# Carrying the running sum of gamma times v: by the token place in SBUF and two passes with ones, in place of three passes with gamma

## What is computed

```python
q = _mlp(x, W1q, b1q, W2q, b2q)
k = _mlp(x, W1k, b1k, W2k, b2k)
v = _mlp(x, W1v, b1v, W2v, b2v)
scores = jnp.einsum('bid,bjd->bij', q, k) / scale
scores = scores * mask
out = jnp.einsum('bij,bjd->bid', scores, v)
...
out = (out - mu) * jax.lax.rsqrt(var + LN_EPS) * ln_w + ln_b
```

## Time and profile before

| | us |
|---|---|
| median of 3 runs | 637.05 |
| lowest and highest | 636.82, 637.2 |
| the profiled execution | 638.8 |
| its span | 637.1 |
| TensorE busy | 608.0 |
| VectorE busy | 432.8 |
| ScalarE busy | 415.0 |
| GpSimd busy | 349.1 |

### The profile page before, as it was taken

How to read it: one execution, slowest core, us unless ns; L and a number is a source line. 1 busy time by engine, 2 the same in 40 slices (tenths; PEclk the granted TensorE clock), 3 DMA queues, 4 the chain that set the end, 5 groups by cost and what they waited for, 6 DMA issues and landing times. The chain is left out here.

```text
span 637.1 us, 12373 instructions
## 1 busy us (share of the span) xinstructions
PE 608.0 (95%) x4100; PEld 559.9 (88%) x4100; DVE 432.8 (68%) x943; ACT 415.0 (65%) x921; POOL 349.1 (55%) x359
## 2 busy tenths in 40 slices
PE   3999999999999999999999999999999999979994
PEld 2879999899999998998998999989999999868883
DVE  3467777776777777767767778797655555337784
ACT  2656677677676676776776766676766666434665
POOL 1536675775766776756767666566433333003443
PEclk9999999999999999999999999999999999999997
DMA  7211112112111120121111110030000000031434
...
DMA packets 30158, 30.21 MB, mean 47 GB/s; under 512 B 6158, under 2 KB 26028, under 8 KB 30124
## 3 DMA queue, kind: packets, MB, share of 16 engines
...
## 5 line engine op out<-in xcount | busy, mean ns | idle before, releaser
L564 ACT ACTIVATE h_hi<-bank,bias_col 128x512 fp32r<-128x512 f32 x96 | 66.4, 692 | 40.0 <-PE bank L690 39.4
L486 POOL TENSOR_TENSOR h_lo<-xn_all,h_hi 128x512 fp32r<-128x512 f32 x32 | 41.6, 1301 | 79.5 <-ACT xn_all L566 79.4
L688 PE MATMUL bank<-xnT_hi,w_hi 128*128 128x512 f32 x192 | 78.4, 408 | 5.5 <-DVE xnT_lo L978 5.2
L690 PE MATMUL bank<-xnT_hi,w_lo 128*128 128x512 f32 x192 | 77.0, 401 | 0.0
L689 PE MATMUL bank<-xnT_lo,w_hi 128*128 128x512 f32 x192 | 76.8, 400 | 0.0
L1037 DVE TENSOR_TENSOR state_lo<-bank,state_hi 128x512 fp32r<-128x512 f32 x57 | 39.1, 685 | 44.2 <-ACT state_hi L605 44.0
L1411 PE MATMUL bank<-xn_all,e_tok 128*128 128x257 f32 x256 | 66.4, 382 | 0.1
L1317 ACT ACTIVATE e_tok<-bank,shift,xinv 128x256 f32<-128x256 f32 x64 | 36.1, 564 | 44.8 <-PE bank L1394 24.2
L1491 DVE COPY ET_all<-bank 128x256 f32<-128x256 f32 (+1 forms) x64 | 27.0, 423 | 53.2 <-PE bank L1405 52.7
L492 POOL TENSOR_TENSOR ktok_lo<-xn_all,ktok_hi 128x512 fp32r<-128x512 f32 x32 | 38.1, 1193 | 44.8 <-ACT ktok_hi L581 44.8
L605 ACT CAST state_hi<-bank 128x512 fp32r<-128x512 f32 x57 | 33.5, 587 | 42.0 <-PE bank L807 42.0
...
## 6 DMA issues: line engine op xcount, KB each, us to landing
...
```

The source lines that it names most:

```text
L486: pool.tensor_tensor(h_lo[:, V_SLOT, m, :], hv[:, m, :], h_hi[:, V_SLOT, m, :].bitcast(F32), ALU.subtract).then_inc(hv_split, 1)
L564: nc.scalar.activation(h_hi[:, h_slot(j, n), m, :], ps, ACT.Gelu, bias=bias(n, m))
L688: nc.tensor.matmul(ps, w[0], xs[0], start=start, stop=False, skip_group_check=shared)
L690: return nc.tensor.matmul(ps, w[1], xs[0], start=False, stop=stop, skip_group_check=shared)
```

## The change

gamma times v is no longer multiplied by TensorE. VectorE keeps, for each of the 128 token places (partitions), the sum over the chunks so far of gamma v at this place: v_sum[:, c] is the sum ahead of chunk c (sum_v; close_sum hands it on to the next group). ScalarE casts v_sum two chunks at a time (round_vsum), GpSimd takes the difference (split_vsum), and `carry` brings the sum over the 128 places into the chunk's own output tile with a matrix of ones, which needs no low part: two matmuls instead of three. The first matmul of a tile now starts it afresh, so preload and mark_out are gone, and TensorE waits for z_ready itself. causal shrinks to one copy. The numbers of instructions: 180 matmuls with gamma become 120 with ones; 56 preloads, 16 gam_hi, 16 gam_lo and mark_out go; 60 sums on VectorE, 32 casts on ScalarE and 32 differences on GpSimd come.

```diff
@@ -282,13 +282,15 @@
...
             ku_rows = asb("ku_rows", [P, KC])
-            gam_hi = asb("gam_hi", [P, GT], F32R)
-            gam_lo = asb("gam_lo", [P, GT], F32R)
+            v_sum = asb("v_sum", [P, GT, D])
+            vsum_hi = asb("vsum_hi", [P, GT, D], F32R)
+            vsum_lo = asb("vsum_lo", [P, GT, D], F32R)
+            ones_r = asb("ones_r", [P, P], F32R)
             bias_rows = asb("bias_rows", [3 * KB, P])
...
             lnb_rows = asb("lnb_rows", [P, D])
-            causal = asb("causal", [P, GT, P])
+            causal = asb("causal", [P, P])
             xT_hi, xT_lo = xnT_hi[0], xnT_lo[0]
...
@@ -497,6 +497,12 @@
...
                                        ALU.subtract).then_inc(v_split, 1)
+
+                def split_vsum(g, m):
+                    pool.wait_ge(vsum_rounded, 2 * g + m + 1)
+                    pair = slice(2 * m, 2 * m + 2)
+                    pool.tensor_tensor(vsum_lo[:, pair, :], v_sum[:, pair, :], vsum_hi[:, pair, :].bitcast(F32),
+                                       ALU.subtract).then_inc(vsum_split, 1)
 
                 def body(g, j, ba, attend=True, project=True, settle=True, more=True):
...
@@ -511,6 +517,8 @@
...
                     if project:
+                        if attend:
+                            split_vsum(a, 1)
                         split_hv(g, 1)
...
@@ -522,7 +530,10 @@
...
                         split_v(g, 0)
+                        split_vsum(g, 0)
                         split_v(g, 1)
+                        if not more:
+                            split_vsum(g, 1)
                     if attend and project:
...
@@ -575,7 +586,6 @@
...
                     act.wait_ge(k_biased, GT * g + GT)
-                    nc.scalar.copy(gam_hi[:, :], k_tok[:, :, D]).then_inc(gam_rounded, 1)
                     for m in range(2):
...
@@ -584,11 +594,10 @@
...
 
-                def preload(ba, i):
-
-                    act.wait_ge(carried, CB * ba + i - 1)
-                    act.wait_ge(z_ready, TB * ba + i + 2 - i % 2)
-                    nc.scalar.copy(out_tile(i % GT), out_tile((i - 1) % GT)).then_inc(preloaded, 1)
+                def round_vsum(g, m):
+                    act.wait_ge(v_summed, GT * g + 2 * m + 1)
+                    pair = slice(2 * m, 2 * m + 2)
+                    nc.scalar.copy(vsum_hi[:, pair, :], v_sum[:, pair, :]).then_inc(vsum_rounded, 1)
 
                 def round_v(g, m):
...
@@ -625,11 +634,9 @@
...
                         round_state(ba, i + 1, tail_hi[1])
-                        preload(ba, i + 2)
                         nc.scalar.activation(warm[:, :], warm[:, :], ACT.Exp).then_inc(table_warm, 1)
...
                         round_masked(a)
-                        preload(ba, i + 3)
                         apply_z(act, a - 1, (ja - 1) % 2, (0, 1))
...
@@ -639,8 +646,6 @@
...
                             round_state(ba, i + 1)
-                        if i + 2 < TB:
-                            preload(ba, i + 2)
 
...
@@ -652,6 +657,8 @@
...
                         follow(0)
+                    if attend:
+                        round_vsum(a, 1)
                     hidden(g, j, WV1, 0)
...
@@ -667,9 +674,12 @@
...
                     round_v(g, 0)
+                    round_vsum(g, 0)
                     if not more:
...
                     round_v(g, 1)
+                    if not more:
+                        round_vsum(g, 1)
                     if not attend:
...
@@ -727,14 +737,6 @@
...
 
-                def mark_out():
-
-                    pe.wait_ge(m_split, KB)
-                    for ps in out_ps:
-                        last = nc.tensor.matmul(ps[:, :], ident[:, :], causal[:, :, :].rearrange("p c n -> p (c n)"),
-                                                start=True, stop=True)
-                    last.then_inc(out_marked, 1)
-
                 def project_k(g, j, t):
...
@@ -780,14 +782,14 @@
...
 
-                def read_state(ba, i, c, p, stop, hi=state_hi, lo=state_lo):
+                def read_state(ba, i, c, p, start, stop, hi=state_hi, lo=state_lo):
                     pe.wait_ge(state_split, CB * ba + i)
...
                         last = split3(out_tile(c), (h_hi[:, p, kb, toks], h_lo[:, p, kb, toks]),
-                                      (hi[:, kb, :], lo[:, kb, :]), False, stop and kb == KB - 1, shared=True)
+                                      (hi[:, kb, :], lo[:, kb, :]), start and kb == 0, stop and kb == KB - 1, shared=True)
                     return last
...
                 def attend_chunk(a, c, start, stop):
@@ -809,34 +811,32 @@
...
 
-                def carry(a, ba, i):
-
-                    c = i % GT
-                    if c == 0:
-                        pe.wait_ge(gam_split, a + 1)
-                    if i > 0:
-                        pe.wait_ge(preloaded, PB * ba + i)
-                    split3(out_tile((i + 1) % GT),
-                           (gam_hi[:, c:c + 1].to_broadcast([P, P]), gam_lo[:, c:c + 1].to_broadcast([P, P])),
-                           (v_hi[:, c, :], v_lo[:, c, :]), False, False, shared=True).then_inc(carried, 1)
+                def carry(a, c, start):
+                    pe.wait_ge(vsum_split, 2 * a + c // 2 + 1)
+                    if isinstance(a, int) and a == 0 and c == 1:
+                        pe.wait_ge(ones_rounded, 1)
+                    nc.tensor.matmul(out_tile(c), ones_r[:, :], vsum_hi[:, c, :], start=start, stop=False,
+                                     skip_group_check=True)
+                    nc.tensor.matmul(out_tile(c), ones_r[:, :], vsum_lo[:, c, :], start=False, stop=False,
+                                     skip_group_check=True)
 
                 def chunk(a, ja, ba, c, p):
                     i = GT * ja + c
-                    if 0 < i < TB - 1:
-                        pe.wait_ge(preloaded, PB * ba + i)
+                    if c % 2 == 0:
+                        pe.wait_ge(z_ready, GT * a + c + 2)
                     if i == 0:
-                        pe.wait_ge(z_ready, GT * a + 2)
                         last = attend_chunk(a, c, True, True)
                     elif c == 0:
-                        read_state(ba, i, c, p, False)
+                        read_state(ba, i, c, p, True, False)
+                        carry(a, c, False)
                         last = attend_chunk(a, c, False, True)
                     else:
-                        attend_chunk(a, c, False, False)
-                        last = read_state(ba, i, c, p, True)
+                        attend_chunk(a, c, True, False)
+                        carry(a, c, False)
+                        last = read_state(ba, i, c, p, False, True)
                     last.then_inc(chunk_done, 1)
...
                         update_state(a, c, i == 0)
-                        carry(a, ba, i)
 
                 def last_chunks(a, ja, ba, p):
...
@@ -845,12 +845,12 @@
                     def update(c):
...
                         update_state(a, c, False)
-                        carry(a, ba, i + c)
 
                     def read(c):
-                        if c < GT - 1:
-                            pe.wait_ge(preloaded, PB * ba + i + c)
-                        read_state(ba, i + c, c, p, False, tail_hi[c], tail_lo[c])
+                        if c % 2 == 0:
+                            pe.wait_ge(z_ready, GT * a + c + 2)
+                        carry(a, c, c % 2 == 0)
+                        read_state(ba, i + c, c, p, False, False, tail_hi[c], tail_lo[c])
 
                     def attend(c):
...
@@ -1007,11 +1007,6 @@
...
 
-                def split_gamma(g):
-                    dve.wait_ge(gam_rounded, g + 1)
-                    nc.vector.tensor_tensor(gam_lo[:, :], k_tok[:, :, D], gam_hi[:, :].bitcast(F32), ALU.subtract
-                                            ).then_inc(gam_split, 1)
-
                 def bias_v(g, j, m):
...
@@ -1019,11 +1014,36 @@
...
 
+                def sum_v(g, j, c):
+
+                    dve.wait_ge(v_biased, 2 * g + c // 2 + 1)
+                    if not (isinstance(g, int) and g == 0):
+                        dve.wait_ge(v_summed, GT * g + c)
+                        dve.wait_ge(vsum_split, 2 * g)
+                    elif c > 0:
+                        dve.wait_ge(v_summed, c)
+                    gamma = k_tok[:, c, D:D + 1]
+                    if j == 0 and c == 0:
+                        last = nc.vector.tensor_scalar(v_sum[:, 1, :], v_tok[:, 0, :], gamma, None, ALU.mult)
+                    else:
+                        last = nc.vector.scalar_tensor_tensor(out=v_sum[:, c + 1, :], in0=v_tok[:, c, :], scalar=gamma,
+                                                              in1=v_sum[:, c, :], op0=ALU.mult, op1=ALU.add)
+                    last.then_inc(v_summed, 2 if j == GB - 1 and c == GT - 2 else 1)
+
+                def close_sum(g, j):
+
+                    if j < GB - 1:
```

(18 more changed lines are left out.)

19 lines of the change are left out of this document (9 added, 10 removed).

## The result

The changed kernel takes 671.12 us (median of 4 runs, 669.15 to 672.79) where the kernel before took 636.93 in the same batch: **1.054 times as long, 95% interval 1.051 to 1.057**. The forecast was 667, in a range of 647 to 676. The profiled execution took 670.57 us, 668.8 of it the span, 31.7 more than the 637.1 of before.

What follows compares the result with a forecast made beforehand. TensorE was taken to bound the attention stage, through chains that must close in time. 15 bodies at a net +2.0 us gave +30 on the profiled 638.8, 668.8, or 667 us as a median; range 647 to 676.

Steps and rivals of the forecast that it cites:

- TensorE's saving, 6.8 us: Attention stage: 60 carries of two matmuls instead of three save 0.113 us each, 0.45 us in a body with four carries.
- Totals do not bind: Attention stage: the added work fills no other engine; by totals alone the change would be worth its 6.8 us.
- The place: TensorE would idle before the read of chunk 1, waiting for state_lo, in some 15 bodies, 2.4 us each.
- Taking turns at the port: VectorE and GpSimd alternate from the first h_lo from hq, two add_ln_b falling in: 5.2 us to the end of state_lo.
- VectorE keeps the port: Rival, chance 0.18: only one add_ln_b falls into the chain, a wait of 1.15 us a body, 650 us in all.
- sums do not take the port: Rival, chance 0.12: only h_lo meets add_ln_b; sums 0 and 2 run earlier, net +1.3 us a body, 657 us.
- The size of the wait: Read of chunk 1: TensorE waits 2.4 us for state_lo, net +2.0 us a body after the 0.45 saved.
- the walk: Queues followed through one body: first gelu 2.1 us late, state_lo done at 225.7 us, wanted by TensorE at 223.27.
- The opening at 0: Before the attention stage: mark_out goes, but the square of mu may come later; 0, with bounds of -1.9 and +1.0 us.
- The body with the scalings: Body before the last: four scalings already cost 0.95 us idle; it would wait some 0.5 us more than the others.
- The closing body "only saves": Closing body: no added wait, only a saving, 9 matmuls to 8.
- The clock "as before": Granted clock: unchanged despite waits of 2.4 us, since it held beside slices with more idle time.

Runs made afterwards that it cites:

- the run of two passes: The kernel before with only the third pass of each carry (gam_lo by v_hi) left out: 631.85 us, ratio 0.990.
- the moved kernels: The changed kernel with operations reordered: only add_ln_b behind split_x, 641.44 us; or sums, casts, differences, add_ln_b and carry all moved, 636.75 us.
- everything moved: The changed kernel with sums behind state_lo, casts behind gelus, differences, add_ln_b and carry later, closing body reordered: 636.75 us, ratio 0.999.

## Why the prediction was right, and where it was not

**TensorE's saving, 6.8 us: right.** 6.1 in the run of two passes, with 0.45 us in a usual body, as forecast, and 0.42 in the moved kernels.

**Totals do not bind: right.** No engine rose over 91%, and the kernel is slower.

**The place: right.** The wait stands at the read of chunk 1, put down to state_lo, once in each of 15 bodies. The cause too: moving the addition of ln_b alone takes 30 us away, and adding only sums to the old kernel brings 27.

**Taking turns at the port: right, and it decided.** "VectorE keeps the port" would have had sum 2 at 0.4 us and one long h_lo; the rows show sum 2 at 1.52 and the h_lo behind it at 1.78, an addition in front of each, so the engine that waits got in between two operations that the other had queued. The Trainium skill, SBUF — State Buffer, Who interferes with whom, says that the two exclude each other; the trace agrees with that (0.48 against 1.52 us for the same sum) and adds the order. The rival "sums do not take the port" fell with the same rows.

**The size of the wait: too large.** Forecast 2.4 us and a net +2.0 a body; measured 1.53 and +1.4 in a usual one (1.14 and +1.3 without close_sum). Two terms of the walk were mis-sized. The first gelu was 2.1 late by the walk and 1.8 in the trace, and the first h_lo from hq began 8.21 us into the body where the walk had it at 8.59. From there to the end of state_lo I had 5.2 us; with close_sum it took 4.8, without 4.4. Two operations were blocked, as in the walk, but by 1.05 and 1.09 us (1.52 less 0.47, 1.78 less 0.69) and not by a whole addition of 1.27 each. The body that I walked has no close_sum, though the walk has one; it stands for a usual body. Over bodies 1 to 14 this is 20 us, 1.5 of them the one body with the lower clock, instead of 28. The net of a usual body is more than the wait in brackets less the saving (1.53 - 0.42 = 1.11 of 1.38), because the bracket starts at the end of the matmul before. From start to start the stop at the read of chunk 1 costs 1.69 us (208.92 - 207.11 less the usual 0.12) and the first matmul behind it 0.11 more (0.23 to the next one); less 0.42 that is 1.38.

**The opening at 0: wrong, +1.5.** mark_out is gone, but sum_mu_squares waits 3.53 us for the square of mu, and the first sum, which I took at the price of a free one, takes 1.42 us where the other three of its form take 0.35. Kernel after, VectorE, GpSimd and ScalarE:

```profile
31.47 1.42 DVE L1027 TENSOR_SCALAR v_sum<-xn_all 128x256 f32<-128x256 f32 x1
31.48 1.27 POOL L498 TENSOR_TENSOR v_lo<-xn_all,v_hi 128x512 fp32r<-128x512 f32 x1
...
32.93 0.62 ACT L600 CAST vsum_hi<-v_sum 128x512 fp32r<-128x512 f32 x1 [2.35 <-DVE v_sum L1027]
```

My upper bound was +1.0; the port was left out of it. From the last matmul of v to the first body it is 5.42 us instead of 3.55, so the change costs 1.9 here; the profile of after had begun its first hidden matmul 0.3 us earlier. Where the first cast stands later (everything moved) it is 3.55 again: leaving mark_out away gained nothing, since the square of mu was due only then.

**The body with the scalings: much too small.** I gave it a wait 0.5 us above the others; it has 4.15, 2.6 above. I did not lay the four scalings beside GpSimd's queue, though the rule that decided the other bodies was on the table. And the sum took the 2.0 of a usual body for it, where my own terms give 1.5: a wait of 2.9, less the 0.95 that was there, less 0.45.

**The closing body "only saves": wrong.** Of the +10.1 of the last two bodies, 3.2 are body 15's longer wait and 3.8 the longer waits of the closing body; with 0.5 saved some 3.6 are left. The clock was 0.62 from 424 to 428, 0.54 from 445 to 450 and 0.78 from 450 to 455, which is an estimated 1.5, 1.2 and 1.1 us of TensorE's busy time; that this is the rest is argued, no run shows it apart. Three sums, two casts and two differences of the last group stand there ahead of the tail states, and the walk never went through it.

**The clock "as before": wrong in small.** The mean went from 0.995 to 0.981, in stretches behind waits of 1.8 to 4.3 us. I argued from slices of 16 us, in which such a gap is averaged away.

So the total is near (31.7 against 30 in the profiles, 34.2 in the medians), but by errors that cancel, which is luck: 8 us too much in bodies 1 to 14, and 9.6 too little in the opening (1.5 against 0) and the last two (10.1 against 2.0). All of the rivals' times are off; 657 for the "sums without port" is nearer to the truth of the usual bodies than my own.
